# Semaphores cleared after half the convolution, and the filters' spread and the first pair's loads cut into six portions

## What is computed

```python
# 1 differential attention: q1, q2, k1, k2 (16 heads of 16), v (16 heads of 32), causal
comb = softmax(q1 k1) - lam * softmax(q2 k2)
out = merge(norm(comb @ v)) @ Wo
# 2 ffn with ternary weights
out = gelu(x @ tern(W1).T + b1) @ tern(W2).T + b2
# 3 convolution: gated linear unit, then 15 taps for each of 16 heads, then W2
w = softmax(conv_shared_weight)
out = conv(a * sigmoid(g), w) @ W2 + b2
# 4 mixture of 16 experts, 2 of them for each row, and two shared experts
out = combine(experts(x), gate) + shared(x)
```

## Time and profile before

| | |
|---|---|
| runs (3) | 3388.02, 3391.98, 3393.28 us; median 3391.98 |
| profiled execution | 3394.89 us, span 3393.1 us, mean granted TensorE clock 0.972 |
| TensorE, VectorE, ScalarE, GpSimd busy | 94%, 78%, 68%, 52% of the span |
| DMA | 396.59 MB, 117 GB/s over the span |

### The profile page before, as it was taken

The page is one execution under the profiler, slowest core; times in us unless marked ns, Lnnn a source line. Parts: engine busy times, 40 slices in busy tenths (PEclk is TensorE's granted clock), DMA queues, the critical chain, the costliest instruction groups (busy, mean ns, idle before and its releaser), DMA issues.

```text
span 3393.1 us, 114047 instructions
## 1 busy us (share of the span) xinstructions
PE 3195.1 (94%) x45534; PEld 2166.2 (64%) x45534; DVE 2660.6 (78%) x6036; ACT 2306.8 (68%) x4989; POOL 1753.5 (52%) x3173
## 2 busy tenths in 40 slices
PE   8989999999999999999999998999989889969988
PEld 6767455555555555555555555888867766648863
DVE  7877889999999999999999982666665548856656
ACT  5656477888888788877778875677665546635533
POOL 1440377777777777777777775111110115646651
PEclk9999799999999999999999998999999989989999
DMA  7797533333333333333333313222143115346658
GB/s 237 247 257 246 99 77 81 85 87 85 82 85 86 86 80 85 84 87 81 79 82 86 88 39 100 75 94 75 50 142 110 50 56 159 122 137 191 198 184 298
DMA packets 380521, 396.59 MB, mean 117 GB/s; under 512 B 121368, under 2 KB 294424, under 8 KB 377816
## 3 DMA queue, kind: packets, MB, share of 16 engines
q1 hardware_dynamic: 365112, 349.32, 37.4%
q0 software_dynamic: 13728, 37.83, 3.1%
q10 hardware_dynamic: 1152, 2.14, 0.2%
HBM read 230.29 MB, written 157.25 MB: 114 GB/s over the span
## 4 chain that ended last, share of the span: by engine, by line
PE 67%; POOL 10%; SPq 6%; DMA 4%; DVE 4%; ACT 4%; issue 4%; POOLq 0%; ACTq 0%; DVEq 0%
PE att_st L716 12%; PE att_pv L784 8%; PE att_ring L744 5%; SPq L690 5%; PE att_ring L716 4%; PE prj_qk L568 4%; PE ffn_hp L1151 3%; PE ffn_ya L1132 3%; PE ffn_yo L1162 3%; PE ffn_hp L2228 3%; POOL att_orms L877 2%; DMA att_ops_more<-att_mpart 2%; PE ffn_ya L1579 2%; POOL att_p L903 2%; PE ffn_ya L2174 2%
## 5 line engine op out<-in xcount | busy, mean ns | idle before, releaser
L831 ACT ACTIVATE att_p<-att_st 128x512 f32<-128x512 f32 (+3 forms) x3072 | 1310.2, 494 | 373.2 <-PE att_st L716 358.1
L917 DVE TENSOR_REDUCE att_mcol<-att_ring 128x1 f32<-128x512 f32 (+1 forms) x2048 | 1225.4, 648 | 94.3 <-PE att_ring L716 49.0
L716 PE MATMUL att_st<-att_ops_more 99*32 99x512 bf16 (+3 forms) x9216 | 700.5, 327 | 25.2 <-DMA att_ops_more<-att_mpart 23.2
L903 POOL TENSOR_SCALAR_AFFINE_SELECT att_p<-att_p 128x512 f32<-128x512 f32 x512 | 324.4, 634 | 336.0 <-ACT att_p L831 322.8
L784 PE MATMUL att_pv<-att_p,att_va_more 128*32 128x512 f32 (+3 forms) x4608 | 483.0, 488 | 4.3 <-POOL att_p L903 3.0
L716 PEld LDWEIGHTS att_st<-att_ops_more 99*32 99x32 bf16 x9216 | 265.6, 96 | 302.5 <-ACT att_p L831 96.1
L744 PE MATMUL att_ring<-att_ops_more 96*32 96x256 bf16 (+5 forms) x6912 | 382.7, 286 | 0.1
L716 PE MATMUL att_ring<-att_ops_more 96*32 96x512 bf16 x3072 | 318.0, 384 | 1.5 <-DMA att_va_more<-values 1.4
L749 PE MATMUL att_ring<-c_mask,c_identb 128*32 128x32 bf16 (+2 forms) x5632 | 296.0, 187 | 0.0
L716 PE MATMUL att_st<-att_ops 99*32 99x512 bf16 (+3 forms) x3072 | 236.4, 327 | 10.1 <-DMA att_ops<-att_mpart 9.8
L744 PEld LDWEIGHTS att_ring<-att_ops_more 96*32 96x32 bf16 x6912 | 169.5, 96 | 100.5 <-DVE att_mcol L917 26.3
(11 more groups left out here) (350 smaller groups left out, 7157.0 us busy)
## 6 DMA issues: line engine op xcount, KB each, us to landing
att_ops_more<-parts SPq DMA_DIRECT2D x1152, 64.0 KB, 3.0
parts<-prj_pt SPq DMA_DIRECT2D x128, 384.0 KB, 3.4
att_ops<-parts SPq DMA_DIRECT2D x384, 64.0 KB, 2.9
moe_work<-moe_rows SPq DMA_DIRECT2D x79, 261.0 KB
values<-prj_vs SPq DMA_DIRECT2D x16, 1024.0 KB, 6.7
heads<-att_ofin SPq DMA_DIRECT2D x128, 128.0 KB, 2.5
ffn_os<-heads SPq DMA_DIRECT2D x16, 1024.0 KB, 4.8
c_xw<-moe_outs SPq DMA_DIRECT2D x16, 1024.0 KB, 10.0
```

The costliest lines, as they stand in the source:

```text
L716: ins = nc.tensor.matmul(out[row:row + VC], stationary[:, row:row + VC], moving, start=start, stop=stop, tile_position=(0, row))
L831: act.activation(pr[:, g % R, b, off:GN], stp[(t * NST + n) % NS][:, off:GN], ACT.Exp, scale=SCALE).then_inc(exp_done, 1)
L903: pool.affine_select(out=d, in_=d, compare_op=ALU.is_ge, fill=0.0, base=0, pattern=[[0, 4], [1, P]], channel_multiplier=-1).then_inc(maske ...
L917: ins = v.tensor_reduce(to[:, h, c, i % HB if c else i:(i % HB if c else i) + 1], of[:, 0:w], AX.X, ALU.max)
```

## The change

The six stores of the spread each take a sixth of the columns of z (682 or 683 elements of each of 128 rows) and stand behind groups 8 to 13, each followed by four of the 24 loads of the first pair; the load of the values is behind the last four. The wait for the spread's landing moves from SyncE's end of the projection into left(), which GpSimd calls too. The clears and C["reused"] move from behind request 14 of the convolution to behind request 7 (B = 8: now numbers 1 to 7, the clears, then 8 to 14). What each wait and clear does is as it was.

```diff
--- before.py
+++ after.py
@@ -333,6 +333,7 @@
     NT = G * NQ
     STATS_AT, NORM_AT, TURN_AT, REST_AT = 0, 2, 4, 6
     SUM_AT, TERN_AT = 3, 5
+    PIECES = 6
     m = Mem(nc, ctx, "prj")
     x = m.sb("x", [P, 2, GT, E])
     xn = m.sb("xn", [P, GT, E])
@@ -368,6 +369,7 @@
 
         eng.wait_ge(parts_ready, NT)
         eng.wait_ge(v_copied, G * GT)
+        eng.wait_ge(C["s_band"], 16 * PIECES)
         batch_stored(eng, B - 1)
 
     def sync(sp, between):
@@ -383,12 +385,14 @@
                 sp.dma_start(pg[g // GB, g % GB, n // EC, n % EC], pt[:, n]).then_inc(part_stored[n], 16)
             sp.wait_ge(v_copied, g * GT + GT)
             sp.dma_start(vg[g // GB, g % GB], vs[:, g % 2].rearrange("p h t v -> p h (t v)")).then_inc(v_stored[g % 2], 16)
-            if g == G // 2:
-                sp.wait_ge(z_ready, K)
-                sp.dma_start(C["spread"], C["z"][:].rearrange("p h l -> p (h l)")).then_inc(C["s_band"], 16)
-                between()
+            if G // 2 <= g < G // 2 + PIECES:
+                piece = g - G // 2
+                if piece == 0:
+                    sp.wait_ge(z_ready, K)
+                cols = slice(piece * H * ZL // PIECES, (piece + 1) * H * ZL // PIECES)
+                sp.dma_start(C["spread"][:, cols], C["z"][:].rearrange("p h l -> p (h l)")[:, cols]).then_inc(C["s_band"], 16)
+                between(piece, PIECES)
         left(sp)
-        sp.wait_ge(C["s_band"], 16)
 
     def gpsimd(pool):
         constants, clear_z, thresholds_set = pre.gpsimd
@@ -675,12 +679,12 @@
             for r in range(2):
                 sp.wait_ge(o_stored[r], 16 * GB * (H // 4) * (b + 1))
 
-        def load(sp, t, s):
-            for n, (a, b) in enumerate(PARTS6):
-                for side, part in ((0, a), (2, b)):
-                    for mat in range(side, side + 2):
-                        sp.dma_start(ops[s][n * D:(n + 1) * D, :, mat, :], pd[t, part, :, :, mat]).then_inc(loaded[s], 16)
-            sp.dma_start(va[s].rearrange("p a t v -> p a (t v)"), vd[t]).then_inc(loaded[s], 16)
+        def load(sp, t, s, piece=0, pieces=1):
+            wanted = [(n, part, mat) for n, (a, b) in enumerate(PARTS6) for side, part in ((0, a), (2, b)) for mat in range(side, side + 2)]
+            for n, part, mat in wanted[piece * len(wanted) // pieces:(piece + 1) * len(wanted) // pieces]:
+                sp.dma_start(ops[s][n * D:(n + 1) * D, :, mat, :], pd[t, part, :, :, mat]).then_inc(loaded[s], 16)
+            if piece == pieces - 1:
+                sp.dma_start(va[s].rearrange("p a t v -> p a (t v)"), vd[t]).then_inc(loaded[s], 16)
 
         def sync(sp):
             def place(t, s):
@@ -964,8 +968,8 @@
                         else:
                             norm(pair, x)
 
-        def load_first(sp):
-            load(sp, 0, 0)
+        def load_first(sp, piece, pieces):
+            load(sp, 0, 0, piece, pieces)
 
         def set_first(pool):
 
@@ -1382,9 +1386,10 @@
 
         @block.sync
         def _(sp):
-            def first_pair():
-                parts_stored(sp, 0)
-                load_pair(sp)
+            def first_pair(piece, pieces):
+                if piece == 0:
+                    parts_stored(sp, 0)
+                load_pair(sp, piece, pieces)
 
             prj.sync(sp, first_pair)
             att.sync(sp)
@@ -1409,10 +1414,11 @@
             ffn.gpsimd(pool, FIRST, LAST)
             cnv.gpsimd(pool, 0, 1)
             ffn.gpsimd(pool, LAST, len(power_order()))
-            cnv.gpsimd(pool, 1, 2 * B - 1)
+            cnv.gpsimd(pool, 1, B)
             for one in passed:
                 pool.sem_clear(one)
             pool.sem_inc(C["reused"], 1)
+            cnv.gpsimd(pool, B, 2 * B - 1)
             moe_first, moe_rest = moe.gpsimd(pool)
             moe_first()
             cnv.gpsimd(pool, 2 * B - 1, 2 * B)
```

## The result

The change makes the kernel faster: 3366.34 us as the median of 4 runs (3360.98 to 3369.61), against 3390.0 us for the kernel before beside it (4 runs, 3384.76 to 3393.28). The ratio is 0.9931, with a 95% interval from 0.9913 to 0.9950: 23.4 us less, between 17 and 29.5. The forecast was 3370.5 us, 21.5 us less than the median of before; the interval of the ratio holds it (3370.5 / 3391.98 = 0.9937). The profiled execution took 3368.22 us with a span of 3366.5 us; before it was 3394.89 and 3393.1.

What follows compares the result with a forecast made beforehand. TensorE is busy 94% of the span, so only waits in the projection and at the convolution's end could go: 14.2 - 0.6 + 7.9 = 21.5 us, giving 3370.5 us against the median of 3391.98, range 3365 to 3379.

Steps and rivals of the forecast that it cites:

- The stall: Projection: ScalarE's copy waits for a late store of the parts; by the chain of waits 14.2 us are lost once.
- The first store, 3 us late: Projection, groups with added transfers: SyncE issues the first store of the parts 3 us later, at 181.5 instead of 178.5.
- The 9.9 us: Projection: time left for the first store to land before ScalarE's copy at 191.37 overwrites its chunk.
- New waiting, 0.6 us: Projection, groups 8 to 13: 0.1 us of new waiting a group, with ends of 0 and 1 us a group.
- 18.2 us of DMA share in 18.34: Projection: transfers a group asks of the DMA engines, 14.9 + 3.3 us, against its 18.34 us; close to full but fitting.
- the excess of the jam, 20 us: Projection: DMA time of the spread and loads, 49.7 us busy less 29.7 for two ordinary groups; 3.3 us a group.
- The clears: End of the convolution: moved clears cost nothing and VectorE's wait for the experts' first rows goes, 7.9 us gained.
- the rival by which it holds: TensorE after the convolution's end: its clock stays at 2.4 GHz after the shorter gap, 2.7 us more gained; chance 0.12.
- each added transfer costs its landing: Projection: five more transfers at no less than 2.5 us each add 12.5 us, giving 3383 us; chance 0.03.
- The too-full engines: Projection: DMA engines too full, so each group gives back about 1 us, giving 3376 us; chance 0.17.
- The slower case: Projection: at highest issue times the first store comes 13 us later; at worst 36 us lost, 3428 us; chance 0.03.
- The experts' rows: End of the convolution: the experts' first rows still come late, losing half or all of 7.9 us; chance 0.06.

Runs made afterwards that it cites:

- the loads whole: Changed kernel with all 25 loads of the first pair behind group 8, the spread still in six pieces; 3369.96 us in one execution.
- the spread whole: Changed kernel with the spread stored in one transfer behind group 8, the loads still in six portions; 3367.01 us in one execution.
- Three portions: Changed kernel with eight loads and a third of the spread behind each of groups 8, 9 and 10; 3363.93 us in one execution.
- the portions alone: Changed kernel with the clears put back behind request 14; 3381.52 us, ratio 0.9970 to the kernel before; again on another chip 3381.36 us, 0.9967.
- the kernel with 24 pieces: Changed kernel with each sixth of the spread cut in four, 24 transfers of 85 KB; 3374.96 us in one execution.
- two portions: Changed kernel with twelve loads and half of the spread behind each of groups 8 and 9; 3376.73 us in one execution.
- the clears alone: Kernel before with only the clears moved behind request 7 of the convolution; 3381.58 us, ratio 0.9976 to the kernel before.

## Why the prediction was right

**The stall (14.2 us forecast, 14.17 measured).** The step from the chain of waits held to the tenth, in all profiles of kernels with six portions (14.16 to 14.21). Its reason held too: the stores come late because of what is issued ahead of them. With the loads whole 10.6 us are back, with the spread whole 1.0, and with no more than a sixth of each ahead of them none.

**The first store, 3 us late (measured 3.9 to 5.4).** Mis-sized, by taking the loads at 0.63 us in the mean. In their old place four took 2.5 us by that mean; now they take 3.16 and 4.54 us. The piece of the spread took 2.50 us, as long on the queue as the whole of it had in the earlier trace rows, which was the upper end of the forecast's 0.47 to 2.50. The 9.9 us shrink by as much, and all landings count, not the median. The store at 221.25 is wanted landed at 229.1: the copy at 191.37, two groups later and shifted by the 1.05 us of this profile. With the median landing of 4.0 us 3.8 us are in hand, with the longest of 6.6 us 1.2 us; by the forecast's numbers it was 6.5 us beyond the median. Three portions, with landings to 7.8 us, are already over the edge by 1.1 us in all. The forecast was right with less room than it claimed.

**New waiting, 0.6 us (measured none), and 18.2 us of DMA share in 18.34 (measured 16.7).** The term that was wrong is the share: I took the excess of the jam, 20 us, as work to be moved. Over groups 8 to 13 the share is 0.91 of 110.1 us against 0.80 or 0.81 in an ordinary group, so the spread and the loads are worth 11 to 12 us, about 2 a group and not 3.3. The earlier trace rows had the hint: at a share of 1.10 only 150 GB/s were moved, against 257 at 0.81 in an ordinary group. So the share in the jam is no measure of what the same bytes take when they are spread out. One group reached 0.99, the forecast's level for all, and still kept its 18.3 us.

**The clears (7.9 us forecast, 8.0 measured at the seam, 7.5 left at the end of the first profile).** The statistics lost their wait whole, the norm came right behind the root of request 14, and the idle time of ScalarE fell to 1.36 us (1.5 forecast). At the new place the clears cost nothing; the cover that the prediction put at 0.6 us is 0.7 by its own rows, and 0.8 measured. The clock fell behind the shorter gap, as the forecast took from the nearest of the earlier trace rows, in all profiles with early clears; the rival by which it holds (2.7 us more) did not come. What I had missed is that the low spell ends 7 to 11 us sooner behind the root than before, which makes the term 7.7 to 9.3 us at the experts' third root: up to 1.4 us of the rival's 2.7 did come. By the experts' last root it is 4.0 to 10.1 us in the eleven profiles with early clears. That is a scatter of the experts' stage: with the clears late, the portions alone stand at +0.1 and -3.0 us there against the kernel before.

**The rivals.** That each added transfer costs its landing (12.5 us for five) is refuted by the kernel with 24 pieces: 23 more transfers than the whole spread, and the late projection at 128.29 us. By the fixed 2.0 us of the Trainium skill ("DMA: Bandwidth & Descriptors", section "Anatomy of one DMA — SWDGE (gpsimd) path"), which it states for transfers issued from GpSimd, an estimate for them is 46 us if the cost of each is added; this case's trace, with transfers issued from SyncE, shows none of it. The same page's rule of 1 MiB or more (section "Bandwidth") would have small pieces move worse; with pieces of 85 KB the stage kept its length, at a DMA share of 0.90 against 0.91. The too-full engines (1 us a group) did not come with six portions. With two portions 6.6 us are lost, but that needs no full engines: the first store behind the second portion is issued some 7.7 us later than with six. The slower case needed four loads at 2.03 us each; the most that four took is 4.54 together in the changed kernel and 6.50 in the one with the spread whole. The experts' rows were not late.

**The sum.** 14.2 - 0.6 + 7.9 = 21.5 us forecast; by the traces 14.2 + 7.5 to 8.0, about 22; by the times 23.4, 22.4 and 21.1 us in three series. In every one the 21.5 lies within the interval. The two terms are shown to be right by the traces; that the times come within 2 us is in part luck, since each series is sure to some 6 us only.

## What to carry to other kernels

When an engine is held up by a store that was issued late, look at what the queue issued ahead of it, and count issue time and not bytes: here 24 small loads (1.5 MB) in front of a store cost 10.6 us, the spread of 2 MB with four of them 1.0 us, and the loads four at a time with a sixth of the spread nothing. Take as slack only what is left after the longest landing. Housekeeping that another engine must see, such as clearing semaphores, belongs where its engine waits anyway, ahead of need; here one request ahead and seven gave the same seam.

## What the runs showed that I had not expected

- A transfer's time on the queue depends on its place more than on its size: right behind the store of the values of an ordinary group the x load takes 2.56 us, the whole spread 2.50, and in the changed kernel each sixth of it 2.50 to 2.68; the x load behind four loads of the first pair takes 0.42 us (1.78 in one group of five). So the portions' issue time is in part the x load's own wait, moved. The forecast had guessed this, but not that the size makes so little of it.
- The same attention, with the same instructions, took 1670.8 to 1688.3 us in 14 profiles. Half a per cent of the kernel's time is scatter in a stage that the change does not touch; two single profiles can't be subtracted without a stage-by-stage balance.
- After 3.61 us of idle time TensorE was at 1.2 GHz, as after 11.62 us, but the low level ended sooner: 15.0 us behind the root of request 14 (12.1 in the clears alone) against 22.4. With that gap taken away and one of 3.90 us behind it the clock fell as well, and of 3 to 4 us about 1 was left at the end of the one profile.
